# Identity products in TensorE's waits, joined remainders of experts and an earlier division in a four-layer decoder

## The chip, the cores and the metric

The kernel runs on one core of one Trainium2 chip. The metric is the device time of one launch in microseconds (us). A launch computes all four rows of the batch, one after the other.

## The reference, cut to what matters

A pre-layernorm decoder of four layers; each layer adds an attention, a second ("cross") mixer and a feed-forward part to `x` of shape [4, 512, 128]. In order these are: a gated delta rule, cross attention over 77 context rows and 16 small experts (layer 0); latent causal attention, cross attention and 8 experts (layer 1); causal attention with normed queries and keys, a cross mixer, and a routed linear attention (layer 2); a state-space mixer, a convolution done by Fourier products, and 8 experts (layer 3). The parts that matter here:

```python
def _L1_ffn_ref(x_bsD, router_DE, w1_eDF, w3_eDF, w2_eFD, ws1_DF, ws3_DF, ws2_FD):
    B, S, D, E, F, K = (4, 128, 128, 8, 352, 1)
    ...
    gates_Ea = jax.nn.sigmoid(masked_aE).T
    routed_in_EaD = jax.lax.stop_gradient(gates_Ea[:, :, None] * x_aD[None, :, :])
    mid_EaF = jax.nn.silu(jnp.einsum('ead,edf->eaf', routed_in_EaD, w1_eDF)) * jnp.einsum('ead,edf->eaf', routed_in_EaD, w3_eDF)
    routed_out_EaD = jnp.einsum('eaf,efd->ead', mid_EaF, w2_eFD)
...
def _L1_attn_ref(...):
    ...
    att = jnp.where(causal[None, None], att, -jnp.inf)
    att = jax.nn.softmax(att, axis=-1)
    y_lat = jnp.einsum('bhqk,bhkl->bhql', att, v_lat)
    y = y_lat @ l2o_w.T + l2o_b
    y = y.transpose(0, 2, 1, 3).reshape(B, T, C)
    return y @ cproj_w.T + cproj_b
```

## The kernel before, in words

One loop of four **passes** runs over the rows of the batch. A pass keeps its row of x (512 tokens by 128 features) in SBUF and goes through twelve **stages**; in the profile's names `l_attn`, `l_xattn` and `l_ffn` stand for the stages of all four layers. Ahead of each stage `Norm.block` (L150 to L210) adds the result of the stage before to the residual (L195), norms it and turns it. A stage is one or more `nc.Block`s: in each, every engine has its own list of instructions, written out by hand, and semaphores tie them together; a block ends when all its engines have come to its end. Weights are fetched into rings a stage ahead by SyncE's queue and are not on any path spoken of here. TensorE works through its list strictly in the written order, so whatever stands ahead of a wait is done before the wait is looked at.

`warm` (L85 to L89) issues `count` **identity products**: a 128x128 bf16 identity times itself, 512 columns wide, into a PSUM bank that nobody reads. The kernel already has 1824 of them in its four passes, put ahead of waits of TensorE.

The places that the change touches:

- `experts_stage` (L225): layer 1 has 8 experts with 352 hidden columns each, 2 x 128 + 96, and a shared expert. Each cut of up to 128 columns is a **tile**: an `up` product (L309), a `gate` product (L310), the silu on ScalarE (L340), a product on VectorE (L399), and four `down` products of 128 columns (L94) one tile later. There are 24 routed tiles and 3 shared ones. The input of an expert is weighed by its gate first (`weigh_input`, L378), from a spread of the gate over the partitions (L298), in a ring of two. Layer 0 puts its 16 experts of 64 columns in pairs instead and weighs the output; TensorE waits for its gates (`gate_ready`) behind 26 identity products.
- `cross_attention_stage` (L0 and L1): four groups of four heads. `shifted(g)` makes the scores (L517, L522) in the same four banks for each group, so it waits until ScalarE's Exp (L558) of the group before has read them; `mix(g)` (L531) multiplies by the values and by ones. Then VectorE divides, in two halves of 256 columns (L597, L599), and TensorE projects each half (L543).
- `causal_attention` (L610, used by layers 1 and 2): a first part finds the maxima (L685 and L688 on TensorE, L770 on VectorE), a second one works through 12 units `u`: scores (L704, L707), Exp (L746), the causal triangle set to zero on GpSimd (L760), products with the values and with ones in strips of 32 columns (L722), and a division (L787, L789). In layer 1 (`shared` false) each of the four groups of heads has its own division; in layer 2 one division ends the part. In layer 1 the next block has four products with `l2o` (L903), ScalarE's bias (L911), and the projection (L94).
- The **preamble of l1_attn** (L822 to L855): a chain of latent product (L832), ScalarE (L864), rotation (L838), VectorE (L877 to L883) for each of eight groups, with the queries first, then four products for the values (L850).
- The **preamble of l2_attn** (L938 to L956), `stage_l3_attn` (waits behind 14, 10 and 12 identity products), and `stage_l3_xattn` (L1411, L1416, then L94 behind VectorE's products).
- The routed linear attention of layer 2 (l2_ffn): the experts' choices and shares are turned into rows of 4 partitions (L1712, L1931) and multiplied out as 4-row products (L1719; the shares again at L1725, four of 384 columns in fp32).

```python
def warm(self, pe, count, bank=OUT):
    for _ in range(count):
        pe.matmul(self.bank(bank), self.ident_bf[:, :], self.ident_bf[:, :].unsqueeze(1).to_broadcast([P, NT, P]),
                  start=True, stop=True)
```

## Time and profile before

| | |
|---|---|
| median of three runs | 4649.6 us (4646.76 to 4651.16) |
| the profiled execution: its own time, its span | 4650.33 us, 4648.7 us |
| TensorE matmuls busy | 3947.6 us, 85% |
| TensorE weight loads busy (beside the matmuls) | 2432.8 us, 52% |
| VectorE, ScalarE, GpSimd busy | 53%, 33%, 18% |
| mean granted clock of TensorE | 0.939 of 2.4 GHz |

The four passes take about a quarter of the span each. Names of the stages below: l0a is layer 0's attention, l0x its cross attention, l0f its experts, and so on; stage l2f is the routed linear attention. A stage's stretch starts where `Norm.block` adds the result before it. PEclk in a view is the granted clock over that stretch: 1.00 is 2.4 GHz, 0.50 is 1.2 GHz. An fp32 matmul is two instructions in the trace, a bf16 one is one.

### The profile page before, as it was taken

The numbers are of one execution on the slowest core, as the hardware profiler recorded it, in microseconds if no ns is written. First come the engines' busy times: TensorE is split into PE (matmuls) and PEld (weight loads), VectorE is DVE, ScalarE is ACT, GpSimd is POOL, SyncE is SP. The second block draws the span as 40 slices with busy tenths as digits, with TensorE's granted clock in tenths as the row PEclk, the third lists the DMA queues.
The fourth block names the chain that finished last, engine by engine and source line by source line (L and its number), as shares of the span: only waits on it lengthen the run. The fifth ranks groups of instructions, "written<-read, shape, count | busy, mean of one in ns | idle before, by whom it ended". The sixth has DMA issues, their size and how long they took to land. (4 is left out here: it accounts for less than half of the span.)

```text
span 4648.7 us, 96577 instructions
## 1 busy us (share of the span) xinstructions
PE 3947.6 (85%) x38308; PEld 2432.8 (52%) x38308; DVE 2458.2 (53%) x6106; ACT 1548.9 (33%) x3480; POOL 824.4 (18%) x1456
## 2 busy tenths in 40 slices
PE   6998787888799879789879987978987997797888
PEld 4883343465587334346558733434655873343465
DVE  6664433554666443455467644345546764434554
ACT  4442222342454222234145422224414442222431
POOL 2430001130243000113024301011302430101120
PEclk9998899999999989999999988999998999899999
DMA  2001000000000100000000010000000001000000
GB/s 82 3 10 51 2 18 18 23 36 26 26 3 12 48 17 3 18 23 36 26 26 3 12 48 19 1 18 23 36 26 26 3 12 48 19 3 16 23 36 28
DMA packets 11005, 105.56 MB, mean 23 GB/s; under 512 B 1148, under 2 KB 5552, under 8 KB 6192
## 3 DMA queue, kind: packets, MB, share of 16 engines
q1 hardware_dynamic: 10544, 99.21, 5.6%
q8 instruction: 314, 5.14, 0.4%
q14 instruction: 147, 1.20, 0.1%
HBM read 98.16 MB, written 1.05 MB: 21 GB/s over the span
## 5 line engine op out<-in xcount | busy, mean ns | idle before, releaser
L88 PE MATMUL psum<-ident_bf 128*128 128x512 bf16 x1824 | 514.9, 421 | 203.8 <-DVE l_attn_peak L770 66.7
L88 PEld LDWEIGHTS psum<-ident_bf 128*128 128x128 bf16 x1824 | 179.8, 106 | 461.5 <-issue 162.8
L3052 DVE TENSOR_TENSOR l_attn_xx<-l_attn_xx,psum 128x256 f32<-128x256 f32 x512 | 204.6, 419 | 208.8 <-PE psum L2655 197.6
L2817 ACT ACTIVATE l_attn_ax<-psum 128x128 f32<-128x128 f32 (+1 forms) x768 | 185.4, 279 | 364.1 <-PE psum L2636 249.4
L399 DVE TENSOR_TENSOR l_ffn_hidden<-l_ffn_silu,psum 128x512 f32<-128x512 f32 (+2 forms) x184 | 126.3, 686 | 325.2 <-ACT l_ffn_silu L340 325.2
L340 ACT ACTIVATE l_ffn_silu<-psum 128x512 f32<-128x512 f32 (+2 forms) x216 | 128.9, 597 | 476.4 <-PE psum L310 476.4
L94 PEld LDWEIGHTS psum<-streamed_weights,l_ffn_hidden 128*128 128x128 f32 (+2 forms) x1728 | 227.0, 193 | 113.6 <-issue 99.2
L2651 PE MATMUL psum<-l_attn_ax,l_attn_xx 64*64 64x64 f32 x5120 | 268.4, 224 | 0.0
L2655 PE MATMUL psum<-l_attn_xx,l_attn_ax 64*64 64x64 f32 x5120 | 261.0, 221 | 0.0
L2941 POOL TENSOR_TENSOR l_attn_part<-l_attn_ab,streamed_weights 128x128 f32<-128x128 f32 x640 | 245.7, 415 | 39.5 <-PE psum L2636 20.3
L770 DVE TENSOR_REDUCE l_attn_peak<-psum 128x4 f32<-128x2048 f32 (+3 forms) x128 | 185.8, 1487 | 125.1 <-PE psum L688 124.5
L94 PE MATMUL psum<-streamed_weights,l_ffn_hidden 128*128 128x128 f32 (+2 forms) x1728 | 231.1, 277 | 9.1 <-DVE l_ffn_hidden L396 5.0
L787 DVE RECIPROCAL l_attn_inverse<-psum 128x512 f32<-128x512 f32 x20 | 67.2, 3358 | 296.1 <-PE psum L722 296.1
L2651 PEld LDWEIGHTS psum<-l_attn_ax,l_attn_xx 64*64 64x64 f32 x5120 | 208.1, 138 | 17.3 <-issue 9.3
L746 ACT ACTIVATE l_attn_prob<-psum 128x2048 f32<-128x2048 f32 (+1 forms) x96 | 152.9, 1593 | 188.8 <-PE psum L707 188.8
L2655 PEld LDWEIGHTS psum<-l_attn_xx,l_attn_ax 64*64 64x64 f32 x5120 | 208.0, 138 | 0.0
L2636 PE MATMUL psum<-l_attn_xx,l_attn_part 64*64 64x64 f32 x5120 | 198.4, 226 | 7.6 <-DVE l_attn_xx L3052 5.3
L2636 PEld LDWEIGHTS psum<-l_attn_xx,l_attn_part 64*64 64x64 f32 x5120 | 176.8, 137 | 35.3 <-issue 16.4
L164 ACT ACTIVATE xnT<-psum 128x256 f32<-128x256 f32 x80 | 30.0, 384 | 443.2 <-PE psum L177 439.0
L760 POOL TENSOR_SCALAR_AFFINE_SELECT l_attn_prob<-l_attn_prob 128x512 f32<-128x512 f32 x128 | 79.7, 635 | 546.9 <-ACT l_attn_prob L746 546.9
L309 PE MATMUL psum<-l_ffn_gated_x,streamed_weights 128*128 128x512 f32 (+1 forms) x320 | 169.4, 611 | 4.5 <-DVE l_ffn_gated_x L378 4.5
L310 PE MATMUL psum<-l_ffn_gated_x,streamed_weights 128*128 128x512 f32 (+1 forms) x320 | 163.4, 592 | 0.0
(523 smaller groups left out, 8006.7 us busy)
## 6 DMA issues: line engine op xcount, KB each, us to landing
streamed_weights<-pack_l_ffn SPq DMA_DIRECT2D x4, 5412.0 KB, 15.4
streamed_weights<-pack_l_ffn SPq DMA_DIRECT2D x4, 3972.0 KB, 12.5
streamed_weights<-pack_l_attn SPq DMA_DIRECT2D x5, 2848.5 KB, 9.5
streamed_weights<-pack_l_xattn SPq DMA_DIRECT2D x4, 2496.0 KB, 8.6
streamed_weights<-pack_l_ffn SPq DMA_DIRECT2D x4, 2192.0 KB, 8.3
streamed_weights<-pack_l_xattn SPq DMA_DIRECT2D x4, 2048.0 KB, 8.5
streamed_weights<-pack_l_ffn SPq DMA_DIRECT2D x4, 1923.0 KB, 8.1
streamed_weights<-pack_l_attn SPq DMA_DIRECT2D x4, 1107.5 KB, 5.1
```

The lines of the kernel that those rows point to most:

```text
L88: pe.matmul(self.bank(bank), self.ident_bf[:, :], self.ident_bf[:, :].unsqueeze(1).to_broadcast([P, NT, P]), start=True, stop=True)
L94: ins = pe.matmul(self.psum[:, OUT, t * P:(t + 1) * P], features[:, t * P:(t + 1) * P], weight, start=first and t == 0, stop=last, skip_gr ...
L309: pe.matmul(m.bank(n % 2)[0:r], w["up"][:, c:c + r], rhs, start=True, stop=True)
L310: pe.matmul(m.bank(2 + n % 2)[0:r], w["gate"][:, c:c + r], rhs, start=True, stop=True).then_inc(up_ready, 1)
L746: act.activation(prob[:, u % SLOTS, :, 0:used(part)], m.psum[:, 0:R, 0:used(part)], ACT.Exp).then_inc(exps_ready, 1)
L770: dve.tensor_reduce(peak[:, g, i, :], m.psum[:, base:base + R, 0:(i + 1) * P], AX, ALU.max, negate=True).then_inc(peak_ready, 1)
L2636: ins = pe.matmul(m.psum[b, p, W * i:W * i + W], part[b, (M * n + l - 1) % 2, p, i, :], xx[b, n % 2, p, X, i, :], start=True, stop=True)
L2651: pe.matmul(m.psum[b, p, P + W * i:P + W * i + W], xx[b, n % 2, p, XT, i, :], ax[b, p, i, :], start=True, stop=True)
L2655: ins = pe.matmul(m.psum[b, p, 256 + W * i:256 + W * i + W], ax[b, p, i, :], xx[b, n % 2, p, XT, i, :], start=True, stop=True)
L2817: act.activation(ax[b, p, :, :], m.psum[b, p, 0:P].rearrange("p (i t) -> p i t", i=2), ACT.Copy).then_inc(ax_ready, 1)
L2941: pool.tensor_tensor(part[:, q % 2, p, :, :], ab[:, n % 2, p, :, 0:W], over_block(w["levels"][:, l, :]), ALU.mult).then_inc(part_ready, 1)
L3052: dve.tensor_tensor(both, both, m.psum[:, p, P:384], ALU.subtract).then_inc(x_less, 1)
```

## The change

1. **Joined remainders** (`experts_stage`, layer 1). A new table `strips(E)` orders the tiles: of each pair of experts, 64 of the 96 remaining columns share one tile of two strips; the last 32 columns of four experts share one of four strips. So 24 routed tiles become 22. A joined tile's up and gate products are done strip by strip, each strip with its own expert's weighed input, so the ring of weighed inputs grows from 2 to 8. The packing of the weights on the host follows.
2. **Identity products**: 181 more in each pass, in the waits of eight stages, as the diff shows them.
3. **The division in halves of columns** (`causal_attention`): the last division is done in two halves of 256 columns, and the products of the last group (in layer 2 of all units) are split at column 256, the far half in other banks. In layer 1 the `l2o` products of the first three groups are now issued at the end of the attention's block (`early`), and one of four is left in the next block. The far product of part 0 of the last group now waits for the division of the group before.
4. **Zero rows** (layer 2's linear attention): the rows of choices and shares are padded from 4 partitions to 128 with zeros by two memsets on GpSimd, and the share products use all 128 rows. ScalarE waits for the memsets.

```diff
@@ -230,24 +230,34 @@
+    shared_by = {}
...
-        tiles += [(e, e * inter + c, r) for e in range(E) for c, r in cuts]
+        if inter % P != 96:
+            tiles += [(e, e * inter + c, r) for e in range(E) for c, r in cuts]
+        else:
+            columns = 0
+            for piece in strips(E):
+                if len(piece) > 1:
+                    shared_by[len(tiles)] = piece
+                tiles.append((piece[-1][0], columns, P))
+                columns += P
...
+    RING = E if shared_by else 2
...
-        gated = sb("gated_x", [P, 2, T])
+        gated = sb("gated_x", [P, RING, T])
@@ -282,7 +292,7 @@
                         if weigh_output:
-                            m.warm(pe, 26, 4)
+                            m.warm(pe, 36, 4)
                         pe.wait_ge(gate_ready, 1)
@@ -303,9 +313,18 @@
-                        rhs = gated[:, g % 2, :]
+                        rhs = gated[:, g % RING, :]
...
+                    if n in shared_by:
+                        for name_, bank in (("up", n % 2), ("gate", 2 + n % 2)):
+                            row = 0
+                            for e, _, rows in shared_by[n]:
+                                ins = pe.matmul(m.psum[row:row + rows, bank, :], w[name_][:, c + row:c + row + rows],
+                                                gated[:, e, :], start=True, stop=True)
+                                row += rows
+                        ins.then_inc(up_ready, 1)
+                        return
@@ -398,6 +417,17 @@
+def strips(E):
...
+    out = []
+    for e in range(0, E, 2):
+        out += [[(e + i, c, P)] for i in range(2) for c in (0, P)]
+        out.append([(e + i, 2 * P, P // 2) for i in range(2)])
+        if e % 4 == 2:
+            out.append([(e - 2 + i, 2 * P + P // 2, P // 4) for i in range(4)])
+    return out
@@ -512,6 +542,7 @@
                     if g >= 1:
+                        m.warm(pe, 10 if g == 1 else 0, 4)
                         pe.wait_ge(exps_ready, g)
@@ -538,6 +569,7 @@
                 for half in range(2):
+                    m.warm(pe, 4 if half else 10, 4)
                     pe.wait_ge(mixed_ready, half + 1)
@@ -651,6 +683,8 @@
         mix_bank = lambda g: 4 if shared else 4 + 2 * (g % 2)
+        far_bank = lambda g: 6 if shared else 4 + 2 * ((g + 1) % 2)
+        HALF = T // 2
@@ -695,9 +729,10 @@
                         wait_consumed(pe, len(steps) - 1)
-                        m.warm(pe, 3, 0)
+                        m.warm(pe, 8, 0)
                         pe.wait_ge(cleared, 2)
                     else:
+                        m.warm(pe, 8 if u == 1 else 0, 7)
                         pe.wait_ge(exps_ready, u)
@@ -715,13 +750,27 @@
-                    for j, c in part:
...
+                    def products(u, j, c, lo, hi, bank):
...
-                                ins = pe.matmul(m.psum[quad(r), mix_bank(g) + n, j * P:T], lhsT,
-                                                prob[:, u % SLOTS, r, c:c + T - j * P],
+                                ins = pe.matmul(m.psum[quad(r), bank + n, lo:hi], lhsT,
+                                                prob[:, u % SLOTS, r, c + lo - j * P:c + hi - j * P],
...
+                        return ins
...
+                    if not shared and g == G - 1 and u % len(parts) == 1:
+                        pe.wait_ge(mixed_ready, G - 1)
+                        products(u - 1, 0, 0, HALF, T, far_bank(g))
+                    for j, c in part:
+                        if not shared and g < G - 1:
+                            ins = products(u, j, c, j * P, T, mix_bank(g))
+                        else:
+                            if j * P < HALF:
+                                ins = products(u, j, c, j * P, HALF, mix_bank(g))
+                            if shared or j > 0:
+                                ins = products(u, j, c, max(HALF, j * P), T, far_bank(g))
@@ -732,6 +781,11 @@
                         mix(u - 2)
+                if early is None:
+                    m.warm(pe, 8, 0)
+                else:
+                    pe.wait_ge(mixed_ready, G - 1)
+                    early(pe)
@@ -780,13 +834,22 @@
-                for g in range(G - 1 if shared else 0, G):
-                    dve.wait_ge(group_mixed, len(parts) * (g + 1))
-                    if g >= 1 and not shared:
-                        dve.wait_ge(mixed_ready, g)
-                    dve.reciprocal(inverse[:, :], m.bank(mix_bank(g) + 1)).then_inc(inverse_ready, 1)
-                    dve.wait_ge(inverse_ready, 1 if shared else g + 1)
-                    dve.tensor_tensor(mixed[:, 0 if shared else g, :], m.bank(mix_bank(g)), inverse[:, :],
+                if not shared:
+                    for g in range(G - 1):
+                        dve.wait_ge(group_mixed, len(parts) * (g + 1))
+                        if g >= 1:
+                            dve.wait_ge(mixed_ready, g)
+                        dve.reciprocal(inverse[:, :], m.bank(mix_bank(g) + 1)).then_inc(inverse_ready, 1)
+                        dve.wait_ge(inverse_ready, g + 1)
+                        dve.tensor_tensor(mixed[:, g, :], m.bank(mix_bank(g)), inverse[:, :], ALU.mult).then_inc(mixed_ready, 1)
+                    dve.wait_ge(mixed_ready, G - 1)
+                for half in range(2):
+                    cols = slice(HALF * half, HALF * half + HALF)
+                    bank = far_bank(G - 1) if half else mix_bank(G - 1)
+                    dve.wait_ge(group_mixed, U - 1 + half)
+                    dve.reciprocal(inverse[:, cols], m.psum[:, bank + 1, cols]).then_inc(inverse_ready, 1)
+                    dve.wait_ge(inverse_ready, (0 if shared else G - 1) + half + 1)
+                    dve.tensor_tensor(mixed[:, 0 if shared else G - 1, cols], m.psum[:, bank, cols], inverse[:, cols],
@@ -832,6 +895,7 @@
                     if 1 <= n <= 2 * G:
+                        m.warm(pe, {1: 7, 2 * G - 1: 7, 2 * G: 10}.get(n, 0))
                         pe.wait_ge(lat_ready, n)
@@ -892,23 +956,26 @@
+        def early(pe):
+            for g in range(G - 1):
+                pe.matmul(m.bank(0), w["l2o"][:, g, :], mixed[:, g, :], start=g == 0, stop=False)
...
-                         lambda g: m.const["ones"][:, 0:32], False, mixed)
+                         lambda g: m.const["ones"][:, 0:32], False, mixed, early)
...
-                for g in range(G):
-                    ins = pe.matmul(m.bank(6), w["l2o"][:, g, :], mixed[:, g, :], start=g == 0, stop=g == G - 1)
-                ins.then_inc(y_psum, 1)
+                pe.matmul(m.bank(0), w["l2o"][:, G - 1, :], mixed[:, G - 1, :], start=False, stop=True).then_inc(y_psum, 1)
...
-                act.activation(q[:, 0, :], m.bank(6), ACT.Identity, bias=w["l2o_b"]).then_inc(y_ready, 1)
+                act.activation(q[:, 0, :], m.bank(0), ACT.Identity, bias=w["l2o_b"]).then_inc(y_ready, 1)
@@ -943,6 +1010,7 @@
                 ins.then_inc(qkv_psum, 1)
+                m.warm(pe, 13, 5)
                 for link in (4, 6, 11):
@@ -953,6 +1021,7 @@
                 ins.then_inc(c_turned, 1)
+                m.warm(pe, 15, 5)
@@ -1265,7 +1334,7 @@
                               stop=True).then_inc(in_psum, 1)
-                m.warm(pe, 14)
+                m.warm(pe, 20)
                 pe.wait_ge(xs_ready, NH)
@@ -1279,9 +1348,9 @@
                     ins.then_inc(x_turned, 1)
-                m.warm(pe, 10)
+                m.warm(pe, 16)
                 pe.wait_ge(dt_logged, 1)
-                m.warm(pe, 12)
+                m.warm(pe, 22)
                 pe.wait_ge(a_ready, 1)
@@ -1405,6 +1474,7 @@
             def _(pe):
+                m.warm(pe, 5)
                 pe.wait_ge(taps_ready, 1)
@@ -1416,6 +1486,7 @@
                 ins.then_inc(wave_psum, 1)
+                m.warm(pe, 10)
                 pe.wait_ge(prod_ready, 1)
@@ -1722,7 +1794,7 @@
                         pe.wait_ge(same_ready, 3)
-                    pe.matmul(m.psum[:, 4 + e, 0:T - P], m.const["pick4"][0:E, e, :], share_rows[:, P:T], start=True,
+                    pe.matmul(m.psum[:, 4 + e, 0:T - P], m.const["pick4"][:, e, :], share_rows[:, P:T], start=True,
                               stop=True).then_inc(share_psum, 1)
@@ -1928,7 +2000,8 @@
                     act.wait_ge(rows_psum, n + 1)
-                    act.activation(rows[:, :], m.psum[0:E, 6 + n, :], ACT.Copy).then_inc(rows_ready, 1)
+                    act.wait_ge(rows_cleared, n + 1)
+                    act.activation(rows[0:E, :], m.psum[0:E, 6 + n, :], ACT.Copy).then_inc(rows_ready, 1)
                 turned(0, "k1T", kT[:, 0, 0, :, :])
```

How TensorE's list changes, at three places. **Preamble of l1_attn**, from its first products on (one row per run of equal instructions); before:

```order
L825 MATMUL psum<-xnT,streamed_weights 128x512 x3
L832 MATMUL psum<-l_attn_qkv,streamed_weights 128x512 x2
L838 MATMUL psum<-l_attn_latent,w_const 128x512
L832 MATMUL psum<-l_attn_qkv,streamed_weights 128x512
L838 MATMUL psum<-l_attn_latent,w_const 128x512
L844 MATMUL psum<-l_attn_rotated,streamed_weights 128x512
```

And changed, where L888, L895, L902 and L908 are the old L825, L832, L838 and L844:

```order
L888 MATMUL psum<-xnT,streamed_weights 128x512 x3
L895 MATMUL psum<-l_attn_qkv,streamed_weights 128x512 x2
L88 MATMUL psum<-ident_bf 128x512 x7
L902 MATMUL psum<-l_attn_latent,w_const 128x512
L895 MATMUL psum<-l_attn_qkv,streamed_weights 128x512
L902 MATMUL psum<-l_attn_latent,w_const 128x512
L908 MATMUL psum<-l_attn_rotated,streamed_weights 128x512
```

Seven identity products stand ahead of the first rotation. Later in the list seven more stand ahead of the seventh rotation and ten ahead of the eighth.

**Layer 1's experts**, from the second tile of an expert to the next expert's spread; before:

```order
L309 MATMUL psum<-l_ffn_gated_x,streamed_weights 128x512
L310 MATMUL psum<-l_ffn_gated_x,streamed_weights 128x512
L94 MATMUL psum<-streamed_weights,l_ffn_hidden 128x128 x4
L309 MATMUL psum<-l_ffn_gated_x,streamed_weights 96x512
L310 MATMUL psum<-l_ffn_gated_x,streamed_weights 96x512
L94 MATMUL psum<-streamed_weights,l_ffn_hidden 128x128 x4
L298 MATMUL psum<-l_ffn_gateT,l_ffn_spread_bf 128x512
```

And changed, behind the fourth expert of the stage (L308, L328, L329 are the old L298, L309, L310; L323 is new):

```order
L328 MATMUL psum<-l_ffn_gated_x,streamed_weights 128x512
L329 MATMUL psum<-l_ffn_gated_x,streamed_weights 128x512
L94 MATMUL psum<-streamed_weights,l_ffn_hidden 128x128 x4
L323 MATMUL psum<-l_ffn_gated_x,streamed_weights 64x512 x4
L94 MATMUL psum<-streamed_weights,l_ffn_hidden 128x128 x4
L323 MATMUL psum<-l_ffn_gated_x,streamed_weights 32x512 x8
L94 MATMUL psum<-streamed_weights,l_ffn_hidden 128x128 x4
L308 MATMUL psum<-l_ffn_gateT,l_ffn_spread_bf 128x512
```

The tile of 96 columns is gone from each expert; a tile of four products in strips of 64 columns stands behind each pair, one of eight in strips of 32 behind each four.

**End of layer 1's attention** with the waits, from the last part of the last group on; before:

```order
L722 MATMUL psum<-l_attn_prob,l_attn_v 32x256 [waits l1_attn_causal]
L722 MATMUL psum<-l_attn_prob,l_attn_v 32x256 x3
L722 MATMUL psum<-l_attn_prob,w_const 32x256 x4
L667 UNCONDITIONAL_BRANCH
L900 UNCONDITIONAL_BRANCH [waits barrier_Pool_Activation_PE_DVE_SP_release]
L903 MATMUL psum<-l_attn_mixed,streamed_weights 128x512 x4
L94 MATMUL psum<-streamed_weights,l_attn_q 128x128 [waits l1_attn_y_ready]
```

And changed (L758 is the old L722):

```order
L758 MATMUL psum<-l_attn_prob,l_attn_v 32x256 [waits l1_attn_causal]
L758 MATMUL psum<-l_attn_prob,l_attn_v 32x256 x3
L758 MATMUL psum<-l_attn_prob,w_const 32x256 x4
L962 MATMUL psum<-l_attn_mixed,streamed_weights 128x512 [waits l1_attn_mixed]
L962 MATMUL psum<-l_attn_mixed,streamed_weights 128x512 x2
L701 UNCONDITIONAL_BRANCH
L969 UNCONDITIONAL_BRANCH [waits barrier_Pool_Activation_PE_DVE_SP_release]
L971 MATMUL psum<-l_attn_mixed,streamed_weights 128x512
L94 MATMUL psum<-streamed_weights,l_attn_q 128x128 [waits l1_attn_y_ready]
```

Three of four `l2o` products stand ahead of the end of the block (L701), where they wait for the divisions of the first three groups; one is left behind it.

## Rows read from the trace of the kernel before

**Rows 1.** The page, part 1: busy time, share and instructions by engine.
```profile
PE 3947.6 (85%) x38308; PEld 2432.8 (52%) x38308; DVE 2458.2 (53%) x6106; ACT 1548.9 (33%) x3480; POOL 824.4 (18%) x1456
```

**Rows 2.** Windows l0x, l1a: stretch, length, busy of five engines, PEclk, DMA share, GB/s.
```profile
346.70:389.20 42.50, 31.23 (x198) 11.08 (x197) 16.90 (x44) 11.16 (x10) 1.95 (x3) 0.88 0.06 25
441.20:581.60 140.40, 108.29 (x782) 44.40 (x781) 68.26 (x94) 31.69 (x31) 12.15 (x19) 0.89 0.09 38
```

**Rows 3.** Two stretches at the lower clock, by windows.
```profile
733.90:737.30 3.40, 3.40 (x11) 1.28 (x13) 0.00 (x0) 0.00 (x0) 0.67 (x2) 0.50 0.00 0
897.80:908.00 10.20, 10.20 (x18) 5.10 (x19) 4.00 (x7) 3.82 (x8) 0.00 (x0) 0.50 0.00 0
```

**Rows 4.** Timeline, l0f, TensorE ahead of the gates.
```profile
401.72 2.75 PE L88 MATMUL psum<-ident_bf 128*128 128x512 bf16 x12
407.11 0.62 PE L288 MATMUL psum<-w_const,l_ffn_gate 128*48 128x128 f32 x4 [2.64 <-DVE l_ffn_gate L371]
```

**Rows 5.** Timeline, l1a, start of the maxima.
```profile
484.11 1.89 PE L88 MATMUL psum<-ident_bf 128*128 128x512 bf16 x8 [1.12 <-PEq L821]
485.92 1.14 PE L685 MATMUL psum<-l_attn_k,l_attn_q 32*128 32x512 f32 x8
```

**Rows 6.** Timeline, l0x, then l1x: start us, us, instructions, idle before, releaser.
```profile
365.46 1.87 ACT L558 ACTIVATE l_xattn_prob<-psum 77x2048 f32<-77x2048 f32 x1
...
382.13 1.76 DVE L597 RECIPROCAL l_xattn_inverse<-psum 128x256 f32<-128x256 f32 x1 [19.50 <-PE psum L531]
384.40 0.71 PE L543 MATMUL psum<-w_l_xattn,l_xattn_mixed 128*128 128x128 f32 x4 [2.34 <-DVE l_xattn_mixed L599]
386.53 1.22 PE L543 MATMUL psum<-w_l_xattn,l_xattn_mixed 128*128 128x128 f32 x4 [1.41 <-DVE l_xattn_mixed L599]
...
599.70 1.87 ACT L558 ACTIVATE l_xattn_prob<-psum 77x2048 f32<-77x2048 f32 x1 [0.65 <-PE psum L522]
601.62 0.67 PE L517 MATMUL psum<-l_xattn_qT,l_xattn_k_of 32*77 32x512 f32 x4 [1.97 <-ACT l_xattn_prob L558]
...
613.46 1.76 DVE L597 RECIPROCAL l_xattn_inverse<-psum 128x256 f32<-128x256 f32 x1 [15.93 <-PE psum L531]
```

**Rows 7.** Stage l0f in the four passes, by windows.
```profile
3867.40:3916.10 48.70, 41.70 (x173) 21.78 (x172) 25.90 (x62) 9.52 (x15) 2.58 (x7) 0.96 0.04 13
...
sum 202.10, PE 174.08 PEld 90.29 DVE 103.51 ACT 38.08 POOL 10.32; mean PE 43.52 PEld 22.57 DVE 25.88 ACT 9.52 POOL 2.58
```

**Rows 8.** Timeline, preamble of l1a.
```profile
452.26 1.12 PE L838 MATMUL psum<-l_attn_latent,w_const 128*128 128x512 f32 x2
```

**Rows 9.** Timeline, l1a, first two units.
```profile
523.73 2.09 PE L704 MATMUL psum<-l_attn_q,l_attn_k 32*128 32x512 f32 x8
528.02 0.93 PE L704 MATMUL psum<-l_attn_q,l_attn_k 32*128 32x384 f32 x8 [1.40 <-ACT l_attn_prob L746]
```

**Rows 10.** Timeline, l1a, products of the last group, its division, the l2o products.
```profile
562.23 1.07 PE L722 MATMUL psum<-l_attn_prob,l_attn_v 128*32 128x512 f32 x8
562.68 0.13 PEld L722 LDWEIGHTS psum<-l_attn_prob,w_const 128*32 128x32 f32 x4 [0.30 <-issue]
...
570.20 0.69 DVE L789 TENSOR_TENSOR l_attn_mixed<-psum,l_attn_inverse 128x512 f32<-128x512 f32 x1
571.28 6.46 PE L903 MATMUL psum<-l_attn_mixed,streamed_weights 128*128 128x512 f32 x8 [4.54 <-PEq L667]
```

**Rows 11.** Timeline, l2f, products of the shares.
```profile
897.78 5.48 PE L1725 MATMUL psum<-l_ffn_share_rows,w_const 4*128 4x384 f32 x8
```

**Rows 12.** Timeline, l3x, start.
```profile
1086.63 1.60 PE L1411 MATMUL psum<-l_xattn_taps,streamed_weights 128*128 128x128 f32 x12 [1.98 <-DVE l_xattn_taps L1436]
```

**Rows 13.** Timeline, l1f, from one expert's spread to the next.
```profile
655.28 0.39 PE L298 MATMUL psum<-l_ffn_gateT,l_ffn_spread_bf 24*128 24x512 bf16 x1
...
663.62 0.39 PE L298 MATMUL psum<-l_ffn_gateT,l_ffn_spread_bf 24*128 24x512 bf16 x1
```

**Rows 14.** Timeline, l2f, products in strips of 64 columns.
```profile
916.48 0.60 PE L1692 MATMUL psum<-l_ffn_v_e,l_ffn_k_out 128*64 128x256 f32 x4
```

22 lines of the change are left out of this document (15 added, 7 removed).

## The prediction

> **What bounds the kernel now.** I read the page first: TensorE's matmuls are busy for 85% of the span [rows 1], so no single stage is starved, and time goes where TensorE works slowly or waits. The windows by stage come second: the granted clock is 0.88 in l0x and 0.89 in l1a [rows 2], and below 1 in most of the others. The windows around single stretches come third. The clock has two levels, 0.50 (1.2 GHz) and 1.00 (2.4 GHz), and the lower one comes behind stretches in which TensorE waited or ran products of few rows: the start of l2a's maxima and 10.2 us of l2f run at 0.50, with TensorE busy throughout [rows 3]. Work that is bound by TensorE takes twice as long there, so a microsecond of such a stretch is worth half a microsecond if the clock stays up. The timeline then tells for each place who waits for whom. SyncE's transfers end no wait in any of them.
>
> **Unit prices.** Twelve identity products take 2.75 us [rows 4], eight 1.89 us [rows 5]: 0.86 / 4 = 0.215 us each at 2.4 GHz. Eight take 1.72 us, and the product of another shape behind them starts 1.81 us after the first, so a change of the array's shape costs 0.09 us [rows 5]. An identity product costs nothing while the wait behind it is longer; beyond that it costs its full 0.215 us, since TensorE keeps to its order. All sums are for one pass, against the profiled execution's own 4650.3 us (0.7 us above the median of the runs, which is nothing here).
>
> *(a) Cross attention.* In l0x the chain from the first Exp to the first reciprocal takes 16.67 us (365.46 to 382.13); in l1x, where the clock stays up, the same chain takes 13.76 us (599.70 to 613.46) [rows 6]. The ten products at g = 1 should give l0x the time of l1x: -2.9. They take 2.16 us, the wait is 1.97 us (the idle time before L517 in l1x) [rows 6]: +0.15. The four projections of the second half take 1.22 us at the lower clock and 0.71 us at the higher [rows 6]; with ten and four products in the waits for the two divisions I take -0.6 in each of the two stages (the rest is in the start of the norm behind), and -0.15 for the norm ahead of l1f. Sum -4.1.
>
> *(b) Gates of l0f.* Ten more products, 2.15 us, fit in the idle 2.64 us before L288 [rows 4]. The stage takes 48.7 us in the pass with a clock of 0.96, and 202.1 us in all four, against 4 x 48.7 = 194.8 if all went like it [rows 7]: -7.3 in all, -1.8 a pass.
>
> *(c) Preamble of l1a.* The seven products at n = 1 stand ahead of L838 at 452.26. The row shows no idle time before it [rows 8]; its chain (rotation, VectorE, ScalarE) sets the pace for the seven groups that follow, so 7 x 0.215 + 0.09 = 1.6 us are exposed. The other 17 lie in waits that exceed them, and give back the clock for the value products, -0.4. Net **+1.2**: here the change loses.
>
> *(d) First units of both causal attentions.* At u = 0, five more products, and its row shows no idle time before the first L704 [rows 9]: +1.1. At u = 1 there are eight, 1.72 + 0.09 us, in an idle time of 1.40 us [rows 9]: +0.3 to 0.4. The first L704 group takes 2.09 us, begun at the lower clock, and the products of the next two units partly follow it [rows 9]: -2.3 for l1a and -2.5 for l2a, of which the first row's gain is the least sure. Net -0.85 and -1.05: -1.9.
>
> *(e) End of l1a.* The far product of part 0 waits for the division of the group before, and the split makes more products of fewer columns: I let the last division end 1.0 us later than now (the row's 570.20 + 0.69 = 570.89). From there to the sum in PSUM stand four `l2o` products, 6.46 us, most of it at the lower clock [rows 10]; one is left, 0.86 us warm, and the three others lie beside the reciprocals. 6.46 - 1.07 = 5.4 gained, 1.0 lost: **-4.4**. Bounds: -3 if the one is done at the lower clock and the division slips by 1.5, -5.4 if nothing slips.
>
> *(f) l2a.* The preamble's 13 and 15 products lie in waits for VectorE; the 3.40 us at 0.50 at the start of the maxima [rows 3] pass in half the time: -1.6. At the end, the halves let the second reciprocal begin on half the columns (-0.6), and eight products keep the clock in about half of the passes (-0.5). Sum -2.7.
>
> *(g) Zero rows in l2f.* L1725 takes 5.48 us for eight instructions at the lower clock [rows 11], in the stretch of 10.2 us at 0.50 [rows 3]. With 128 rows instead of 4 the columns are the same, so is its length at a given clock. If the fuller products hold the clock up, nearly the whole stretch halves: **-4.9**, since all of it is TensorE's. The two memsets lie before a wait of GpSimd's for VectorE and ScalarE reads them late: 0. Bounds: 0 (the rows do not matter for the clock) and -5.1.
>
> *(h) l3_attn and l3x.* The 22 added in l3_attn lie under ScalarE's and VectorE's chains: 0. In l3x the five before the taps end after the taps are ready: L1411 waits until 1086.63, 0.34 us after VectorE starts the taps [rows 12], and I take it 0.8 later. The clock of 0.92 that two of the passes have there is worth about as much over four passes: 0 net.
>
> *(i) Experts of l1f.* One expert's three tiles and a spread take 8.34 us [rows 13]: a tile is (8.34 - 0.5) / 3 = 2.61 us, TensorE without a pause. Two tiles fewer: -5.2. A joined tile is as long as a full one if its strips run side by side. In the attention eight products in strips of 32 columns start at 562.23 and take 1.07 us, with the next four weight loads under them [rows 10], so four fp32 strips of 512 columns pass in the time of one; in l2f four instructions in strips of 64 columns and 256 columns take 0.60 us, two at a time [rows 14]. Each joined tile changes the array's shape in and out, 2 x 0.09 to 0.12 us; six tiles: +1.4. Net **-3.9**. What a full emptying of the array would cost is bounded by the 0.39 us that one bf16 product of 512 columns lasts [rows 13] less the 0.215 us until the next one starts: 0.17 us. A rule of the Trainium skill ("TensorEngine Tiling (Array Packing)", Key Properties) speaks against the joined tiles: changing the tiling mode drains TensorE. By that rule every change would cost the 0.17, and this item would be -3.2 and the whole 4563; the row's 0.09 [rows 5] says less, and the sum goes by the row.
>
> **Sum:** -4.1 - 1.8 + 1.2 - 1.9 - 4.4 - 2.7 - 4.9 + 0 - 3.9 = -22.5 us a pass, -90 in all: **4560 us**.
>
> **Rivals.**
> *R1, weight loads of strips are not hidden.* All strips of a joined tile use all 128 rows. If each load held the array for the 0.13 us of [rows 10], a tile of two strips would add 8 x 0.13 = 1.04 and one of four 16 x 0.13 = 2.1 us; four and two of them are +8.3 a pass, 4593, less the changes of shape already counted: about **4588**. For it: strips in four different shapes follow each other here for the first time. Against it: the loads under the products in [rows 10]. The Trainium skill ("TensorE: Matmul & The Clock Gate", Part 3) has this rule: a weight load overlaps running matmuls only when the row group differs. By that rule the time is the 4588 just given; the loads of this trace, which lie under products of the same rows, speak against it. In the worst form the strips run one after the other, +17 a pass (4 x 1.7 + 2 x 5.1), **4628**. Chance 0.12 together.
>
> *R2, the clock does not follow.* The identity products could leave the clock as it is, because the fall is caused by something before them. Then (a), (b), (f) and (g) vanish, (c) and (d) cost 1.6 and 2.8, and (e) and (i) stay at about -8.3: with the halves' -0.6 some -4.5 to -2 a pass, **4636 to 4642**, within 0.2% (9.3 us, what a measurement of this kernel can tell from no change) or just outside. For it: l1a at 0.89 in spite of identity products [rows 2]. Against it: the stretches at 0.50 lie behind waits without such products. Chance 0.05.
>
> *R3, slower: the products overrun their waits.* TensorE does 181 more a pass, 181 x 0.215 = 39 us. The waits are sized for the higher clock; wherever a wait is shorter than in the rows (as at n = 1 and u = 0) the products stand on the path, and all engines behind them wait. Gains without any overrun are 28 us a pass (22.5 + 5.5 counted as overrun), so it decides from 28 / 39 = 72% exposed; all exposed, +11 a pass: **4694**. For it: three places where I already see it. Against it: the waits of [rows 4] and of the divisions are longer than the products. Chance 0.03.
>
> **Numbers.** The forecast has 0.80. Its own uncertainty: (g) 0 to -5.1, (e) -3 to -5.4, (i) -2.7 to -5.2, the clock terms of (a), (d) and (f) half or one and a half of what I took (about 4.5 each way), and other stretches at 0.50 in the same stages that may go too, up to -3. Not all fall on one side; I take +8 and -6 a pass: 4536 to 4592, which takes in R1's milder form. Faster by over 0.2%: 0.80 + 0.12 + half of R2 = 0.94; the same 0.03; slower 0.03.
>
> **What would show it.** Right: L1725's eight instructions in about 2.8 us and no 0.50 behind it; the first reciprocal of l0x 13.8 us after the first Exp; one `l2o` product after the block's end and ScalarE's bias about 1.1 us after it; joined tiles of 2.6 to 2.9 us; PEclk of l1a and l2f at 0.95 or more. Wrong: joined tiles of 3.7 us and more (R1); the same PEclk by stage as before (R2); waits of VectorE or ScalarE for TensorE that begin behind identity products (R3).

## The result and the profile after

The changed kernel takes 4626.28 us (median of five runs, 4621.99 to 4649.26) against 4649.6 us: that is 23 us less by the medians, and 16 by the ratio of the runs, 0.9965 (interval 0.995 to 0.998), where 90 less were forecast. Both medians are of five runs. The runs of the changed kernel spread over 27 us, those of the kernel before over 4 here and over 10 to 15 on the chips of the experiments. The profiled execution took 4649.26 us (span 4647.5), the slowest of its five; the comparison of places below is between one execution of each kernel.

The page of the changed kernel, engines and identity products:

```profile
PE 4067.9 (88%) x39736; PEld 2510.2 (54%) x39736; DVE 2453.8 (53%) x6114; ACT 1541.9 (33%) x3472; POOL 827.9 (18%) x1464
...
L88 PE MATMUL psum<-ident_bf 128*128 128x512 bf16 x2548 | 668.5, 401 | 200.7 <-DVE l_attn_peak L824 65.7
```

Against [rows 1] TensorE is busy for 120 us more, 724 more identity products among it (154 us busy), and the mean granted clock rose from 0.939 to 0.949. From the clock, the time at 1.2 GHz went from 2 x (1 - 0.939) x 4648.7 = 567 us to 2 x 0.051 x 4647.5 = 474 us. So 93 us less were spent at the lower clock in this execution, and its span is 1.2 us shorter. That is the first hint: much of what ran at the higher clock now was not what the time hung on.

Windows by stage of the first pass in the changed kernel (columns as in [rows 2]): l0x, l0f, l1a, l2x, l2f.

```profile
347.00:386.00 39.00, 32.90 (x224) 12.31 (x222) 16.86 (x43) 11.15 (x10) 1.95 (x3) 1.00 0.06 27
386.00:437.30 51.30, 45.11 (x183) 23.61 (x182) 25.89 (x62) 9.51 (x15) 2.58 (x7) 0.93 0.04 11
437.30:577.20 139.90, 112.37 (x848) 47.92 (x847) 68.47 (x96) 31.68 (x31) 12.15 (x19) 0.93 0.09 37
816.00:871.10 55.10, 47.20 (x249) 20.36 (x248) 34.34 (x50) 14.16 (x20) 1.09 (x1) 0.94 0.02 6
871.10:1022.40 151.30, 137.08 (x1059) 96.57 (x1057) 79.10 (x191) 68.43 (x147) 48.70 (x57) 0.91 0.05 20
```

And the last two stages before:

```profile
823.20:874.90 51.70, 45.25 (x250) 18.87 (x249) 34.28 (x49) 14.17 (x20) 1.09 (x1) 0.97 0.03 6
874.90:1025.90 151.00, 136.70 (x1059) 95.24 (x1057) 79.23 (x192) 69.00 (x147) 47.80 (x55) 0.92 0.05 20
```

l0x went from 42.5 to 39.0 us at full clock. But l2x, in which not one line was changed, grew by 3.3 us in each pass. The timeline of the places on which the forecast rested, in the changed kernel (line numbers are its own: L902, L739, L971 and L1797 are the old L838, L704, L903 and L1725):

```profile
448.30 1.67 PE L88 MATMUL psum<-ident_bf 128*128 128x512 bf16 x7
449.81 1.02 PE L902 MATMUL psum<-l_attn_latent,w_const 128*128 128x512 f32 x2
...
519.22 3.46 PE L88 MATMUL psum<-ident_bf 128*128 128x512 bf16 x8 [0.79 <-DVE l_attn_peak L824]
522.61 1.14 PE L739 MATMUL psum<-l_attn_q,l_attn_k 32*128 32x512 f32 x8
...
571.50 1.10 PE L971 MATMUL psum<-l_attn_mixed,streamed_weights 128*128 128x512 f32 x2 [1.22 <-PEq L701]
572.63 0.69 ACT L978 ACTIVATE l_attn_q<-psum,streamed_weights 128x512 f32<-128x512 f32 x1 [10.23 <-PE psum L971]
...
661.16 1.94 PE L323 MATMUL psum<-l_ffn_gated_x,streamed_weights 128*64 128x512 f32 x8
663.03 1.16 PE L94 MATMUL psum<-streamed_weights,l_ffn_hidden 128*128 128x128 f32 x8
664.12 1.92 PE L323 MATMUL psum<-l_ffn_gated_x,streamed_weights 128*32 128x512 f32 x16
...
893.95 2.85 PE L1797 MATMUL psum<-l_ffn_share_rows,w_const 128*128 128x384 f32 x8
```

What to see there: the joined tiles' up and gate products last 1.94 and 1.92 us, and one joined tile takes 2.96 us from start to start (661.16 to 664.12, with the down products of the tile before in it); the share products take 2.85 us instead of 5.48 [rows 11]; one `l2o` product stands behind the end of the block, and ScalarE's bias 1.1 us behind it; and the eight products at u = 0 of l1a take 3.46 us, because that place is at 1.2 GHz. Of the signs that the prediction named, PEclk of l1a and l2f failed: it was to be 0.95 or more and is 0.93 and 0.91. A joined tile is just over the 2.9 us that it was allowed. There is no 1.2 GHz right behind L1797, but it comes at the 41st us of the stage.

At u = 0 of l2a the three products of the kernel before ran at 2.4 GHz in all four passes, and the eight of the changed one at 1.2 GHz. The first pass of each:

```profile
772.38 0.82 PE L88 MATMUL psum<-ident_bf 128*128 128x512 bf16 x3 [0.79 <-DVE l_attn_peak L770]
```

```profile
764.66 3.59 PE L88 MATMUL psum<-ident_bf 128*128 128x512 bf16 x8 [0.79 <-DVE l_attn_peak L824]
```

By term, forecast against the local change and against the change of the whole stage in the four passes (from the traces; a stage runs from one norm's statistics to the next):

| term | forecast, a pass | local change | change of the stage's span, four passes |
|---|---|---|---|
| (a) l0x | -3.35 | -2.9 (first Exp to reciprocal 16.67 to 13.76) | -3.4, -3.4, -4.8, -3.4 |
| (a) l1x | -0.75 | -0.3, or +1.1 where it starts at 1.2 GHz | +1.1, -0.3, +1.1, +1.1 |
| (b) l0f | -1.8 | no 1.2 GHz behind the gates, but at its 7th us in three passes | -0.7, -1.6, 0.0, +2.6 |
| (c), (d), (e) l1a | +1.2, -0.85, -4.4 | +1.3; +1.0 to +2.7 at u = 0; -4.2 | -0.6, -5.5, -1.3, -0.5 |
| (d), (f) l2a | -3.75 | -1.6 at the start, +2.6 to +2.9 at u = 0 | -0.5, +0.2, -1.1, -0.2 |
| l2x | 0 | no edit | +3.3, +3.3, +3.3, +3.3 |
| (g) l2f | -4.9 | -5.2 at its 34th us (-3.5 in one pass) | +0.4, +2.8, +3.2, +3.8 |
| (h) l3x | 0 | +0.6 | +0.6, -1.0, -1.0, +0.6 |
| (i) l1f | -3.9 | -3.4 | -3.3, -3.6, -3.3, -3.6 |
| l3f | 0 | no edit | +1.7, +1.7, +1.6, +1.7 |
| l0a | 0 | no edit | +0.5, +1.2, +2.6, +1.0 |

The local change at u = 0 is that of the time from the start of the last maximum to the first Exp: 4.5 to 5.5 us in l1a's first pass, 2.9 to 5.7 us in l2a's. The local prices of (a) in l0x, (c), (e), (g) and (i) came within 0.5 us; (d) did not. Between these two executions 89 us of the forecast are missing (67 between the medians). By stage, over the four passes: l2f 30, l2a 13, l2x 13, l1a 8, l0f 8, l3f 7, l1x 6, l0a 5. So 25 us are in three stages that no edit touched. Some 23 us are term (d), in l1a and l2a, which is taken up below.

### The profile page after: what moved, and what is told of

It is laid out like the page before. It is cut to its first block and busy times, and to the rows that moved or that the text cites. A ratio compares the mean times of both kernels' runs of the same rounds, so it can differ in the third digit from the quotient of the medians.

```text
span 4647.5 us, 99405 instructions
## 1 busy us (share of the span) xinstructions
PE 4067.9 (88%) x39736; PEld 2510.2 (54%) x39736; DVE 2453.8 (53%) x6114; ACT 1541.9 (33%) x3472; POOL 827.9 (18%) x1464
## 3 DMA queue, kind: packets, MB, share of 16 engines
HBM read 97.64 MB, written 1.05 MB: 21 GB/s over the span
## 5 line engine op out<-in xcount | busy, mean ns | idle before, releaser
L88 PE MATMUL psum<-ident_bf 128*128 128x512 bf16 x2548 | 668.5, 401 | 200.7 <-DVE l_attn_peak L824 65.7
L88 PEld LDWEIGHTS psum<-ident_bf 128*128 128x128 bf16 x2548 | 244.6, 103 | 544.1 <-issue 162.7
L359 ACT ACTIVATE l_ffn_silu<-psum 128x512 f32<-128x512 f32 (+1 forms) x208 | 124.1, 597 | 471.5 <-PE psum L329 417.8
L94 PEld LDWEIGHTS psum<-streamed_weights,l_ffn_hidden 128*128 128x128 f32 (+1 forms) x1664 | 215.2, 191 | 113.9 <-issue 102.5
L3016 POOL TENSOR_TENSOR l_attn_part<-l_attn_ab,streamed_weights 128x128 f32<-128x128 f32 x640 | 245.7, 415 | 39.5 <-PE psum L2711 20.3
L824 DVE TENSOR_REDUCE l_attn_peak<-psum 128x4 f32<-128x2048 f32 (+3 forms) x128 | 186.1, 1487 | 119.1 <-PE psum L722 118.4
L94 PE MATMUL psum<-streamed_weights,l_ffn_hidden 128*128 128x128 f32 (+1 forms) x1664 | 223.4, 277 | 8.4 <-DVE l_ffn_hidden L415 5.0
L2504 DVE SCALAR_TENSOR_TENSOR l_attn_conv<-psum,streamed_weights,l_attn_conv 128x511 f32<-128x511 f32 (+2 forms) x192 | 140.8, 747 | 16.5 <-ACT l_attn_conv L2445 12.0
L186 POOL TENSOR_TENSOR residual<-residual,w_columns 128x512 f32<-128x512 f32 x20 | 21.8, 1091 | 706.8 <-DVE xn L203 706.8
L739 PE MATMUL psum<-l_attn_q,l_attn_k 32*128 32x512 f32 (+3 forms) x1024 | 107.4, 492 | 41.6 <-ACT l_attn_prob L800 39.1
```

The lines of the kernel that those rows point to most:

```text
L94: ins = pe.matmul(self.psum[:, OUT, t * P:(t + 1) * P], features[:, t * P:(t + 1) * P], weight, start=first and t == 0, stop=last, skip_gr ...
L359: act.activation(silu[0:r, n % 2, :], m.bank(n % 2)[0:r], ACT.Silu).then_inc(silu_ready, 1)
L824: dve.tensor_reduce(peak[:, g, i, :], m.psum[:, base:base + R, 0:(i + 1) * P], AX, ALU.max, negate=True).then_inc(peak_ready, 1)
L2504: ins = dve.scalar_tensor_tensor(out=later, in0=m.psum[:, chunk_bank(n), 0:T - 3 + i], scalar=w["conv_w"][:, ORDER[n], i:i + 1], in1=later ...
L3016: pool.tensor_tensor(part[:, q % 2, p, :, :], ab[:, n % 2, p, :, 0:W], over_block(w["levels"][:, l, :]), ALU.mult).then_inc(part_ready, 1)
```

## The experiments

Three theories. **A**: the fall to 1.2 GHz does not belong to the edited waits; it comes somewhere in a stretch in which TensorE waits or runs thin products (of few rows or columns), and which instructions it hits depends on the moment the stage starts. **B**: the parts add up and some were mis-sized. **C** (rival R3): the identity products stand in the way. Ratios are against the kernel before, run on the same chip beside each; 0.001 is 4.6 us, and the changed kernel itself has 0.9965.

Times of stages come from one traced execution of each kernel. The traced one of the changed kernel is its slowest, so differences by stage against it come out too large in sum: the traces of no_overrun and of the changed kernel differ by 65 us, their medians by 37.

### The four parts alone

Each is the kernel before with one part of the change (for the division, `early` is in and the eight products at the end are not; for the products, all 181 are in).

> The kernel before with the joined remainders of the experts alone. Theory A (each local price was right; what was lost is that stretches at the lower clock come back at other places of the program): l1f is 3.4 us shorter in each pass as in the changed kernel, but the stages behind it begin 3.4 us earlier relative to the passes' ends and may meet the lower clock elsewhere, so the total lies between -5 and -20 us against before. Theory B (parts simply add up and some are mis-sized): -13.8 us in all (4 x 3.45), every other stage within 0.3 us of before.

Measured: 0.9992 (0.9983 to 1.0001), 4646.32 us. l1f is 3.0 to 3.6 us shorter in each pass, 13.3 in all, and the traced span 5.8. Unedited stages took the rest: l0f -1.6 in one pass and +3.3 in another, l3x +1.6 twice, l2f -1.0 once and +1.0 twice. The total, 3 us less, is below what either theory said (5 to 20, or 13.8).

> The kernel before with the zero rows of the routed linear attention alone. Both theories: the chain of that stage is 5.2 us earlier at its 34th microsecond. Theory A: part of it is given back in the same stage by a stretch at 1.2 GHz that before lay elsewhere, so the stage gains 0 to 5 us by pass, in all 0 to -20 us, and passes differ from each other. Theory B: the 5.2 us reach the end of the stage in every pass, -21 us in all.

Measured: 0.9998 (0.9989 to 1.0007). In all passes l2f's first copy of k_out comes 3.8 us earlier (26.65 us into the stage instead of 30.43), and its end only 0.1 to 1.1 us: the stretches at 1.2 GHz lay at 22.9 to 33.1, 46.8 to 50.2, 91.2 to 94.6 and from 118.5 or 138.9 us on; they now lie at 39.9 to 46.7, 60.4 to 67.2, 118.4 to 128.7 and 142.3 to 145.7. The chain is 5.2 us earlier at the stage's 34th us, as expected. Theory B's -21 us is refuted; the local gain is real and given back inside the stage. A had also said that the passes would differ from each other; they do not.

> The kernel before with the division in halves and the three early l2o products alone, no identity product added. From the last Exp of l1_attn to ScalarE's bias behind the l2o products: 15.4 us before, 11.3 in the changed kernel; expected 11.3 here too. l2a: second reciprocal -0.6 us. Theory B: -4.2 - 0.6 = -4.8 us a pass, -19 in all. Theory A: the same -4.2 at that place, but the norm and the scores behind it may fall to the lower clock (l1x of the changed kernel is 1.1 us longer in three passes), in all -8 to -19.

Measured: 1.0037 (1.0023 to 1.005): **slower**, and outside both expectations. The last Exp to the bias takes 11.3 us instead of 15.4, as expected, and l1a gained 2.6 to 4.3 us in every pass. l2f, untouched, changed by +7.2, +6.3, -1.3 and +4.0 us. Its first and third pass in this kernel:

```profile
872.70:1030.90 158.20, 145.05 (x1059) 100.80 (x1058) 79.10 (x191) 68.99 (x147) 47.78 (x55) 0.86 0.05 18
3197.60:3348.30 150.70, 136.55 (x1059) 94.17 (x1058) 79.43 (x192) 68.98 (x147) 47.76 (x55) 0.92 0.05 20
```

The same 1059 instructions of TensorE take 158.2 or 150.7 us. The busy time of VectorE, ScalarE and GpSimd is the same within 0.4 us; the granted clock is what differs (0.86 and 0.92).

> The kernel before with all 181 identity products added a pass, and none of the other three parts. Forecast by my terms: cross attentions -4.1, gates -1.8, preamble of l1_attn +1.2, first units -1.9, l2a preamble and end -2.1, l3x 0: -8.7 a pass, -35 in all. Theory A: l0x and the start of l2a gain as forecast (-3.4 and -1.6), but the first unit of l1_attn and l2_attn costs 2 us each, since its eight products run at 1.2 GHz, and l2x and l0f meet the lower clock where they are bound by TensorE; the sum is 0 to +25 us. Theory C (the products themselves are in the way): the waits behind them begin late by more than 5 us a pass, +20 or more, with the granted clock no lower than forecast.

Measured: 1.0006 (0.9997 to 1.0015). l0x is 3.4 us shorter in each pass, and the stretches at 1.2 GHz are fewer (clock 0.956). But l1a changes by +1.8, -0.8, +0.2 and +0.8, l2a by +0.2 to +1.4, l3f by +1.7 to +1.8, and l1f by +1.4 to +1.6 in three passes. My terms for the products, -35 us, are wrong by their whole amount; C's mark (+20 or more) was not reached either. A's range was met, but not by the stages it named: l2x kept its 51.7 us and l0f was no longer in any pass.

By their ratios the four alone give -4, -1, +17 and +3 us, which is +15 in sum; together they give -16 (by the ratio) to -23 (by the medians). They don't add, so terms that were each measured alone would not have given the total either.

### What the overrunning products cost

> The changed kernel without the identity products whose wait is too short: the seven at n = 1 of l1_attn's preamble, five of the eight at u = 0 of both causal attentions, the five ahead of the taps. Local expectations from the two traces: the preamble chain of l1_attn 1.3 us earlier, the first Exp of both attentions 2 us earlier where the products run at 1.2 GHz (but L704 behind them perhaps 0.9 slower), the taps 0.6 to 0.8 earlier. Theory B and C: -3 to -4 us a pass, -12 to -16 in all, about 4612. Theory A: the local gains as stated, but other stages change by several us in either direction without any edit; total -20 to +15.

```diff
-                        m.warm(pe, {1: 7, 2 * G - 1: 7, 2 * G: 10}.get(n, 0))
+                        m.warm(pe, {2 * G - 1: 7, 2 * G: 10}.get(n, 0))
...
-                        m.warm(pe, 8, 0)
+                        m.warm(pe, 3, 0)
...
-                m.warm(pe, 5)
                 pe.wait_ge(taps_ready, 1)
```

Measured: 0.9879 (0.9861 to 0.9896), 4589.11 us: 37 us less than the changed kernel, where A said at most 20 less and B and C 12 to 16: outside all three. In the traces l1a is 2.9 to 6.2 us shorter. l2f is 8.0 to 8.4 us shorter in three passes and 3.7 longer in one, with no edit. l3x is 0.5 to 0.6 and l3f behind it 1.7 us shorter in every pass; in no_u0, which keeps the five products ahead of the taps, l3x is as in the changed kernel and l3f in three of four passes. So these five seem to cost some 2.2 us a pass, where 0.8 was forecast; no run took them out alone.

> The changed kernel without the seven identity products at n = 1 of l1_attn's preamble alone. The third latent copy of the preamble 1.3 us earlier in every pass (as in the run without all overrunning products). Theory D (the seconds gained by that run come from the overruns themselves: 1.3 a pass here, 2 a pass and attention at u = 0, 0.6 at the taps): -5 us in all. Theory A (most of it came from stretches at 1.2 GHz that moved off TensorE-bound work): anything from -25 to +5, with the difference lying in stages that were not edited, above all l2f.

Measured: 0.9961 (0.9948 to 0.9975), 4631.36 us. This is the changed kernel's own ratio, though the chain at n = 1 is 1.3 us earlier in every pass. The interval is too wide to tell theory D's 5 us from nothing.

> The changed kernel with three instead of eight identity products at u = 0 of both causal attentions alone. Where they run at 1.2 GHz the first Exp comes 2 us earlier after the last maximum (9.2 us in l1a, now), and L704's first group takes 2.1 instead of 1.1 us, net -1.1; at 2.4 GHz -1.1. Theory D: -1.1 a pass and attention, -9 in all. Theory A: -25 to +5, with the difference in stages that were not edited.

Measured: 0.9878 (0.9863 to 0.9893), 4594.27 us. Five products less at each u = 0 give as low a ratio as all three removals together. The first Exp comes 1.1 us earlier in l1a and l2a where the clock there is the same, as both theories said (9 us in all). The measured gain, 32 us by the medians, is more than A's range (at most 25) and far more than D's 9; the largest part of it in the traces is l2f, 3.1 to 7.9 us a pass.

### Filling the pauses that the faster clock opened

In the changed kernel l2x falls to 1.2 GHz some 7 us after its start. Before, the norm ahead of it ran largely at 1.2 GHz, its 15 identity products filled it without a pause, and the work behind ran at 2.4. Timeline of l2x's first products, before and then in the changed kernel, there with the norm ahead:

```profile
829.78 1.98 PE L1088 MATMUL psum<-ctxT,streamed_weights 128*128 128x77 f32 x16 [1.22 <-PEq L3269]
831.59 1.92 PE L1041 MATMUL psum<-xnT,streamed_weights 128*128 128x512 f32 x4
```

```profile
818.78 1.47 PE L88 MATMUL psum<-ident_bf 128*128 128x512 bf16 x6 [1.36 <-DVE norm_tmp L117]
820.34 1.10 PE L177 MATMUL psum<-w_const,xn 128*128 128x128 f32 x4
822.66 3.55 PE L1157 MATMUL psum<-ctxT,streamed_weights 128*128 128x77 f32 x16 [1.22 <-PEq L3344]
826.01 3.70 PE L1110 MATMUL psum<-xnT,streamed_weights 128*128 128x512 f32 x4
```

At 2.4 GHz the same 15 products leave 1.36 us idle in the middle and the products behind take 3.55 + 3.70 us instead of 1.98 + 1.92. Whether the pause is the reason, the next run tests.

> The changed kernel, with six more identity products in the first wait and four more behind the transposes of the two norms ahead of l0f and l2x. In the changed kernel those norms run at 2.4 GHz, finish their 15 products early and leave TensorE idle, and the stage behind falls to 1.2 GHz while TensorE bounds it. Theory A (the clock falls because of these pauses, and moves from place to place): l2x goes from 55.0 back to 51.7 us or less in all passes, l0f from 51.3 to 48.7 in all passes; -3.3 and -2 us a pass at those stages; the total -10 to -25 us against the changed kernel (about 4600 to 4620), less if l2f behind it takes it back. Theory C (identity products are in the way): each product costs 0.2 us, +4 us a pass at most, l2x and l0f longer.

```diff
-                    m.warm(pe, 9, 2)
+                    m.warm(pe, 15 if more else 9, 2)
...
                     ins.then_inc(self.xn_turned, 1)
+                if more:
+                    m.warm(pe, 4, 2)
```

Measured: 0.9918 (0.9901 to 0.9936), 4612.56 us, in A's range. l2x takes 52.2 us in all passes (2.8 less), l0f 49.2 in all. Each is 0.5 us above the value that A expected. With the pause filled, the fall in l2x is gone in all four passes, so the pause is part of its cause. It isn't all of it: in no_u0, which left this norm alone, l2x went to 53.4 us as well.

> The changed kernel with five identity products behind the three early l2o products, in the 1.2 us in which TensorE waits for the last division and the end of the block. Theory A: the stretch at 1.2 GHz from the 136th microsecond of l1_attn in three of four passes is gone: projection L94 1.2 instead of 1.9 us, l1x 38.3 to 38.6 instead of 39.7; -1.4 to -2 us in those passes at that place, and unforeseeable shifts elsewhere of up to 10 us in all. Theory C: 0 to +1 us a pass.

Measured: 0.9939 (0.9927 to 0.9952), 4617.9 us. l1a is 2.5 to 3.1 us shorter in three passes and l1x 0.3 to 1.4 there; in the fourth they are 0.5 and 1.1 us longer. l2f is 3.1 to 7.7 us shorter in all four, without an edit.

> The changed kernel with six identity products ahead of the 24 products of two columns in the routed linear attention (its last tile of tokens). They lie on TensorE's path: +1.3 us a pass at 2.4 GHz. Theory A: the fall to 1.2 GHz that follows these thin products (from the 119th microsecond of the stage in all passes) is shorter or gone; the stage goes from 151.4 to 155.2 us to 147 to 151 us; total -5 to -20. Theory C: only the cost, +5 us in all.

Measured: 0.9973 (0.9964 to 0.9982), 4635.32 us: 4 us more than the changed kernel by the ratio. A had 5 to 20 less; C's 5 more is what came. l2f takes 150.6, 151.1, 151.1 and 158.2 us: shorter by 0.8 to 4.0 in three passes and 3.4 longer in the last. Whether the products helped there, or the stage's starts did, this run doesn't tell.

> The changed kernel without the overrunning products, with the longer norms ahead of l0f and l2x and with the five products at the end of l1_attn: three edits whose runs each beat the changed kernel, by 37, 14 and 8 us. If they add up, 4567; by theory A they do not, since they work on the same stretches (l2f and l1a improved in all three runs without an edit there): 4570 to 4595, with l0f at 48.7 to 49.2, l2x at 52.2 and l1x at 38.3 to 38.6 in all passes.

Measured: 0.992 (0.9907 to 0.9934), 4614.39 us, above A's range (4570 to 4595) and far above the sum (4567). l2x and l0f are as expected (52.2 and 49.2), l1x is not (39.5 us for 38.3 to 38.6). The kernel is slower than without overruns alone (0.9879): l2f takes 155 us in all passes instead of 146.8 in three. Two edits that each gained on the changed kernel lose 19 us when the third is already there.

> As the kernel with these three edits, with the longer products in the norms of all stages but the first. Stretches at 1.2 GHz begin 6.7 us into l1a, l2f and l0f and 12.9 us into l1x in the run without overruns; theory A: those go, another -1.5 to -3 us a pass, 4560 to 4585. Theory C: where a norm itself runs at 1.2 GHz, 21 products take 9 us instead of 6.4 and delay it by up to 2.6 us; +5 to +20 us, above the kernel with three edits.

Measured: 0.9873 (0.9858 to 0.9888), 4595.08 us, 10 us above A's range. l2f takes 151.4 to 151.9 us. It has the highest mean clock of all kernels (0.963 in the traced run, 0.97 in its fastest, which took 4583.36 us) and is not the fastest.

> The changed kernel without the overrunning products, with the longer products of the norm ahead of l2x alone. The stage l2x goes from 55.0 and 53.4 us to 52.2 in all passes, -1.2 to -2.8 each. Theory B: -6.4 in all, 4583. Theory A: l2x as said, and l2f behind it, which then starts 1.2 to 2.8 us earlier, at anything from 146.8 to 158.4 us a pass: 4580 to 4620.

Measured: 0.9883 (0.9868 to 0.9898), 4604.79 us. l2x takes 52.2 and 52.3 us, 1.1 to 2.8 less, as said. l2f behind it takes 158.5, 148.7, 151.4 and 154.8 us where it took 155.1 and three times 146.8. So by the ratio the 6 us gained in l2x are more than given back.

> The changed kernel without the overrunning products and with the five products at the end of l1_attn. They filled the wait there (l1x -1.4 and -0.3 us, L94 -0.7) in the run that added them alone. Theory A: local -1 us a pass, the total 4575 to 4625, since l2f starts at other moments. Theory B: -8 as alone, 4581.

Measured: **0.9842** (0.9828 to 0.9856), 4578.94 us beside 4655.85 for the kernel before on that chip: the fastest kernel here, 77 us under before. l2f takes 146.8, 146.8, 147.2 and 146.8 us. The time is also what B said (4581), but not for B's reason: against no_overrun l1a is 0.4 to 2.2 us longer and l1x shorter in one pass only, while l0f, where nothing changed, is 2.6 us shorter in three passes and l2f 8.3 in one.

> The best kernel so far (without the overrunning products, with the five at the end of l1_attn: 0.984 of before) without the zero rows. Locally the 10 us stretch at 1.2 GHz around the share products comes back, +5.2 us at the 34th microsecond of l2f. Theory B: +21 us in all, 4600. Theory A: the later part of l2f changes as well; alone, the zero rows gave only 1 us of the stage in before. The stage ends at 150 to 158 us instead of 146.8 to 147.2; total 4590 to 4625.

Measured: 0.9941 (0.9925 to 0.9958), 4622.44 us. Without the zero rows the same kernel is 1% slower: l2f takes 157.2, 155.4, 150.5 and 157.2 us. So the rows, which gave next to nothing to the kernel before, are worth 3.3 to 10.4 us of l2f a pass here, up to twice their local price. The total is 44 us longer, which is in A's range and twice B's 21 us.

### A pure delay

These decide between A and B. VectorE gets one instruction more ahead of the norm before l2f, whose result nobody uses; nothing in l2f is edited. In the spans of the stages the added instruction counts to l2x.

```diff
+                if delay:
+                    dve.reciprocal(m.xn[:, 0:delay, :], m.ident.unsqueeze(1).to_broadcast([P, delay, P])).then_inc(self.delayed, 1)
+                    dve.wait_ge(self.delayed, 1)
                 if add:
```

> The changed kernel without the overrunning products (the reference for this run, 4589 us), with a pure delay in each pass: one reciprocal of 128 columns on VectorE ahead of the norm before l2f, some 0.9 us (1.75 us for 256 columns in the trace). Nothing in l2f or behind it is edited. In the reference l2f takes 146.8 us in three passes and 155.1 in one. Theory A (which stretch of a stage meets 1.2 GHz depends on when the stage starts, not only on its own instructions): the span of l2f, measured from its start, changes by 2 us or more in at least two passes. Theory B (each stage has its own time): every stage within 0.5 us of the reference, the total +4 us.

Measured: 0.9883 (0.9868 to 0.9899), by the ratio no more than the delay itself, as B has it. But the stages moved, which B excludes: l2f takes 153.0, 153.0, 153.3 and 153.0 us instead of 155.1 and three times 146.8, so 6.2 to 6.6 more in three passes and 2.1 less in one, and l0f 2.6 us less in three passes.

> As the run before it, with a delay of 256 columns, 1.8 us in each pass. Theory A: l2f again between 146 and 158 us, another value than with half the delay in at least one pass; the total between +0 and +45 us against 4589. Theory B: +7 us in all, l2f as in the reference.

Measured: 0.992 (0.9907 to 0.9934), by the ratio 19 us over no_overrun for 7.0 us of added instructions. l2f takes 155.5, 153.4, 155.5 and 155.5 us.

> The kernel before with the pure delay of 0.95 us ahead of the norm before l2f, which in the changed kernel without overruns raised l2f from 146.8 to 153.0 us. It tells whether the kernel before depends on the starts of its stages as much. Theory A: l2f, 151.0 and 152.0 us in before, ends at another value in at least two passes by 1 us or more, total -10 to +30 against before. Theory B: l2f within 0.5 us, total +4.

Measured: **1.01** (1.0085 to 1.0115), 4690.48 beside 4647.13 us: 43 us more for 3.8 us of added instructions, beyond even A's range. The added instruction, then l2f in the first two passes, and between them the stretch of the first that makes the difference:

```profile
L194 DVE RECIPROCAL xn<-w_const 128x128 f32<-128x128 f32 x4 | 3.8, 953 | 11.0 <-PEq L3284 11.0
```

```profile
877.80:1041.40 163.60, 149.06 (x1054) 103.33 (x1053) 79.07 (x192) 68.88 (x147) 47.76 (x55) 0.83 0.05 17
991.90:1022.60 30.70, 29.81 (x161) 22.23 (x160) 10.79 (x32) 6.12 (x18) 3.40 (x4) 0.50 0.01 2
2048.50:2202.30 153.80, 138.34 (x1054) 95.39 (x1053) 79.18 (x192) 68.88 (x147) 47.77 (x55) 0.90 0.05 18
```

The first pass spends 30.7 us on end at 1.2 GHz where TensorE is busy for 29.8, with products of which many are thin. Two of its rows there, and the same instructions in the fastest kernel:

```profile
990.99 4.48 PE L1742 MATMUL psum<-l_ffn_low_b,streamed_weights 64*128 64x512 f32 x6
...
997.20 1.23 PE L1649 MATMUL psum<-l_ffn_qg,l_ffn_kg 64*128 64x128 f32 x8
```

```profile
970.11 2.74 PE L1810 MATMUL psum<-l_ffn_low_b,streamed_weights 64*128 64x512 f32 x6
...
973.77 0.71 PE L1717 MATMUL psum<-l_ffn_qg,l_ffn_kg 64*128 64x128 f32 x8
```

The delay also makes TensorE wait 0.95 us longer ahead of l2f, and that wait could be what changes the clock, and not the moment. The trace of before_delay speaks against it: its first and third pass have the same delay, and l0x to l2x take the same time in both, each within 0.05 us. The stretches at 1.2 GHz in the first 94 us of l2f are the same too, within 0.1 us. Yet l2f takes 163.6 us in the first and 153.8 in the third. Each pass works on another row of the batch, but that isn't the reason either: on the same rows, l2f took 151.0 and 152.0 us in these two passes of the kernel before, and 150.5 in all four of products_alone.

So the core of theory A holds, for the kernel before too: the same instructions behind the same stages take different times, with nothing left here that differs but the moment at which they run, and the granted clock differs with it. B is refuted by the delays and by the four parts alone. C holds for the products at u = 0 and, with less, for those ahead of the taps. A is no forecast, though: its ranges for the total missed in eight of the runs (tiles_alone, division_alone, no_overrun, no_u0, variance_products, kept_best, all_norms, before_delay). At which moment the clock falls or comes back, and so which start of a stage is a good one, was not settled: no run varied the thin products of l2f themselves, or delayed a stage by many small steps.

## Why the prediction was wrong

The direction was right and the size was not: 23 us less for 90, far above the range's upper end of 4592.

*Steps that held.* (a) for l0x: 13.76 us for the chain, and the stage 3.4 us shorter for 3.35. (c): +1.3 for +1.2, and the cost of 7 products was read from the row. (e): from the last Exp to the bias 15.4 us before, 11.25 after, -4.2 for -4.4. (g) as a local price: L1725 went from 5.48 to 2.85 us, and the chain is 5.2 us earlier for 4.9. (i) is near: -3.4 for -3.9. The loads of strips that R1 feared were hidden. R1 named a rule of the Trainium skill ("TensorE: Matmul & The Clock Gate", Part 3) by which they would not be; the trace speaks against it here, since sixteen instructions in strips of 32 columns last 1.92 us with their loads. A joined tile takes 2.96 us against 2.61 for a full one, and R1's prices would have made it 3.65 or 4.7. (R1's 0.13 us was the span of four loads and not of one, so its price was read high.) What a joined tile costs more, 0.35 us, is not the 0.2 that I took from [rows 5]; it is the 2 x 0.17 us that the prediction gave as the bound for emptying the array at each change of shape. With that bound the item is -3.2, with the row's price -3.9, and the stage shows -3.3 to -3.6.

*The term that was mis-sized:* (d), forecast at -0.85 us in l1a and -1.05 in l2a. I priced the five products more at u = 0 at 0.215 us each, from rows at 2.4 GHz, and they ran at 1.2 GHz. In l1a's first pass eight products take 3.46 us where three took 1.46, so 2.0 us instead of 1.1, and L704 got back 0.95 of it. In l2a the place was at 2.4 GHz before and fell to 1.2, so reading the clock of the old row would not have been enough: 3.59 us where three took 0.82. The gain from the clock in the next units, most of the -2.3 and -2.5, did not come: from the first Exp to the last, l1a took 0.9 to 1.1 us more in three passes and 0.4 less in one, l2a 0.6 less in three and 2.2 less in one. In all, (d) was +16 us over the four passes in the trace where -8 stood. Taken out, the five products are worth 32 us by their run, most of it by what they moved.

*The step that failed:* the "Sum". It adds local gains and gives them to the end of the pass, as though what follows took its own fixed time. The runs show that it does not. l2f takes 150.5 to 163.6 us in the kernels without the zero rows and 146.8 to 158.5 in those with them, with the same instructions of its own each time (the run with six added products aside). A delay of 0.95 us a pass made the kernel before 43 us slower. Four parts of -4, -1, +17 and +3 us give -16 to -23 together. My uncertainty for the clock ("half or one and a half", 4.5 us a pass) was taken only over the edited stretches and counted nothing for the others, though [rows 7] showed 48.7 us for l0f in one pass and 202.1 in four. The differences between passes would still have said too little: l2f took 151.0 or 152.0 us in the four passes before. The allowance for "other stretches at 0.50 in the same stages that may go too, up to -3" saw only one side: they also come, and in other stages. (h) is a small case of it: l3x came out as forecast over the four passes, and l3f behind it is 1.7 us longer in each.

*The rivals.* R2 (the clock does not follow) was wrong as put: l0x ran at full clock, and 93 us less were spent at 1.2 GHz. But its time, 4636 to 4642, came nearer than my forecast, since the clock fell elsewhere; that is luck, not its mechanism. (Its own -4.5 us a pass gives 4632, not 4636.) R3's overruns happened where the prediction saw them. At n = 1 the cost was the forecast one, at u = 0 about twice its price, and at the taps 0.6 us with 1.7 more in l3f behind.

## What to carry to other kernels

Where a program runs partly at the lower clock, a local gain is a gain only if the stages behind it are looked at too: compare the span of every stage in every pass, edited or not. Take the spread of equal code over passes as the least uncertainty of any forecast; here an unedited stage went well beyond it. Test an edit with a pure delay of the same size beside it: if the delay alone moves the time by more than itself, single edits can't be judged one at a time, and edits have to be tried in combination. Trace more than one execution where the times of one kernel spread over 27 us. Put identity products only where the wait is longer than the products at the *lower* clock: a place that ran at 2.4 GHz before the change can be at 1.2 GHz after it.

## What the runs showed of the hardware that was not expected

- A stretch at 1.2 GHz can last while TensorE is busy: 30.7 us on end with TensorE busy for 29.8 (before_delay, first pass). The same instructions begun at another moment ran at 2.4 GHz in part: six of L1742 took 4.48 us there and 2.74 in no_overrun_end. What brings the clock back was not shown.
- The same program takes different times with the same stages ahead: l2f 163.6 and 153.8 us in the first and third pass of before_delay, behind stages that agree within 0.05 us.
- A fixed number of identity products fills less at the higher clock: the 15 of the norm ahead of l2x leave no pause there when it runs largely at 1.2 GHz, and 1.36 us at 2.4 GHz, and the stage behind then fell (l2x, 51.7 to 55.0 us). With ten products more it took 52.2 us.
- A higher mean clock is not a shorter time: 0.963 with 4606 us (all_norms), 0.962 with 4577 us (no_overrun_end), 0.956 with 4650 us (products_alone), all of the traced runs, and 0.939 with 4650 us before.
- Products in strips of 32 columns, each with its own input and its own weights from the same 128 rows, run side by side with their loads hidden: 16 instructions of 512 fp32 columns in 1.92 us.
